# An eight-core attention and ternary-FFN layer on Trainium2: the loads of the down-projection weights are issued from GpSimd's queue instead of SyncE's and ScalarE's

## The reference, cut to what matters

```python
x = _layernorm(x + attn(x, Wq, bq, Wk, bk, Wv, bv, Wo, bo))     # 16 heads, 4 kv heads, RoPE, causal
# x: (2, 4096, 2048) float32; the FFN, on the normalised x:
def _quant_weight(w):                       # ternary weights
    scale = mean(|w|) + 1e-5
    return clip(round(w / scale), -1, 1) * scale
def _quant_act(x):                          # 8-bit activations, one scale a row
    scale = max(max|x|, 1e-5) / 127
    return clip(round(x / scale), -128, 127) * scale
gate = sigmoid(bitlinear(x, w_gate))        # w_gate, w_up: (8192, 2048)
up   = bitlinear(x, w_up)
h    = gate * up
y    = bitlinear(h, w_down)                 # w_down: (2048, 8192)
out  = _layernorm(x + y)
```

## Time and profile before

| | us |
|---|---|
| median of 3 runs | 6902.17 |
| the profiled execution, its own time | 6898.83 |
| its span on core 2, the slowest | 6897.1 |
| spans of the 8 cores | 6846.7 to 6897.1 |
| stage 5 on core 2, from the first weight DMA to the last `hscr` | 4077.4 to 5418.1 |
| PE busy in the whole span | 3070.9 (45%) |
| DVE busy | 2943.2 (43%) |
| ACT busy | 1663.0 (24%) |
| POOL busy | 386.1 (6%) |

### The profile page before, as it was taken

One profiled execution on the slowest core, in us unless ns is written; L12 is line 12 of the kernel. 1 busy time (PEld: TensorE's weight loads), 2 busy tenths in 40 slices (PEclk: granted clock), 3 DMA queues, 4 the chain that ended last, 5 costly groups with the idle time before them and its releaser, 6 DMA issues. The chain is left out here.

```text
span 6897.1 us, 49237 instructions; the slowest of 8 cores (6846.7 to 6897.1 us)
## 1 busy us (share of the span) xinstructions
PE 3070.9 (45%) x14187; PEld 1466.2 (21%) x14445; DVE 2943.2 (43%) x4502; ACT 1663.0 (24%) x2590; POOL 386.1 (6%) x747
## 2 busy tenths in 40 slices
PE   0014443133333445555546115777768344444442
PEld 0001111011112223333322002333323121222121
DVE  0015554365776555544431432434344433333333
ACT  0002222121223333333310211211112333333322
POOL 0001110121100000000000000000001000000000
PEclk9996776566555555555557557888889677777776
DMA  9977663677654333222224225665665502222202
GB/s 106 109 93 98 99 100 54 101 108 114 161 181 144 128 110 101 97 87 83 74 74 105 76 77 136 157 155 163 159 159 148 132 25 56 58 55 54 49 22 97
DMA packets 735830, 708.01 MB, mean 103 GB/s; under 512 B 607312, under 2 KB 607312, under 8 KB 705616
## 3 DMA queue, kind: packets, MB, share of 16 engines
q0 software_dynamic: 94768, 276.88, 21.0%
q1 hardware_dynamic: 580640, 268.57, 17.4%
q10 hardware_dynamic: 60160, 159.40, 7.3%
HBM read 545.28 MB, written 201.33 MB: 108 GB/s over the span
## 5 line engine op out<-in xcount | busy, mean ns | idle before, releaser
L1390 PE MATMUL gps<-wTg,xqTf 128*128 128x512 bf16 x1966 | 771.8, 393 | 340.3 <-DVE hb L1429 340.0
L1393 PE MATMUL ups<-wTu,xqTf 128*128 128x512 bf16 x2048 | 801.4, 391 | 52.5 <-DMA wTu<-wu_q 46.2
L950 PE MATMUL avp<-ptb,vsb 128*128 128x128 bf16 x2304 | 337.3, 301 | 705.4 <-DVE ptb L940 705.4
L398 DVE TENSOR_REDUCE asum<-mstage 128x1 f32<-128x1024 bf16 x384 | 451.0, 1214 | 269.4 <-DMA mstage<-wg 84.3
L1629 PE MATMUL dn<-wdT,hqT 128*128 128x512 bf16 x1998 | 537.2, 432 | 35.5 <-DVE acc L1648 21.1
L940 DVE COPY ptb<-ptp 128x512 bf16<-128x512 bf16 x576 | 243.8, 423 | 599.8 <-PE ptp L926 599.8
L999 ACT ACT_TABLE_LOAD x128 | 164.2, 1283 | 1182.7 <-remote 824.9
L465 PE MATMUL kps<-wkT,xtg 128*128 128x512 bf16 x491 | 227.0, 462 | 475.3 <-DMA xtg<-xkv_bf 475.1
L1415 ACT ACT_TABLE_LOAD x128 | 164.2, 1283 | 1101.1 <-DVE sgb L1404 1101.1
L926 PE MATMUL ptp<-ident,pnb 128*128 128x128 bf16 x2304 | 360.8, 311 | 136.0 <-DVE pnb L1028 134.3
L950 PEld LDWEIGHTS avp<-ptb,vsb 128*128 128x128 bf16 x2304 | 200.3, 127 | 842.4 <-issue 842.4
(11 more groups left out here) (228 smaller groups left out, 4097.5 us busy)
## 6 DMA issues: line engine op xcount, KB each, us to landing
mstage<-wg POOLq DMA_DIRECT2D x128, 256.0 KB, 6.6
mstage<-wu POOLq DMA_DIRECT2D x128, 256.0 KB, 5.9
mstage<-wd POOLq DMA_DIRECT2D x128, 256.0 KB, 5.4
wfsta<-wg SPq DMA_DIRECT2D x32, 1024.0 KB, 6.0
wfsta<-wg ACTq DMA_DIRECT2D x32, 1024.0 KB, 5.9
wg_q<-tbuf5a POOLq DMA_DIRECT2D x64, 512.0 KB, 5.7
wfsta<-wu SPq DMA_DIRECT2D x32, 1024.0 KB, 5.9
wfsta<-wu ACTq DMA_DIRECT2D x32, 1024.0 KB, 4.8
```

What stands on the lines that cost most here:

```text
L398: mt_red[t] = SM["vMi"].inc(v.reduce_sum(asum[:, t:t + 1], mstage(t)[:, 0:cw], AX.X, apply_absolute_value=True))
L950: last = te.matmul(avp[:, (u % 2) * 512:(u % 2) * 512 + 128], vsb[:, kb * KV + kvh * HD: kb * KV + kvh * HD + HD], ptb(gpar)[:, b * 128:(b ...
L1390: te.matmul(gps[:, qo:qo + 512], lhs, wTg(c)[:, j * 512:(j + 1) * 512], start=(j == 0), stop=(j == DC - 1))
L1393: last = te.matmul(ups[:, qo:qo + 512], lhs, wTu(c)[:, j * 512:(j + 1) * 512], start=(j == 0), stop=(j == DC - 1))
```

## The change

A set of four semaphores (`tfg`) is added. `fac_alloc` takes a flag; for stage 5 it is set, for stage 3 (which uses the same `emit_tern` for the gate and up weights) it isn't. With the flag, every load of a tile, even and odd, is issued by POOL and counted on `tfg` instead of `tf`. The number of buffers (four), the tiles, DVE's work and its place don't change.

```diff
-    def fac_alloc(stack, tag, nd=4):
+    def fac_alloc(stack, tag, nd=4, swdge=False):
         ...
+        FAC["swdge"] = swdge
@@ emit_tern
+        ld_sems = SP["tfg"] if FAC["swdge"] else SP["tf"]
         for t in range(lo, hi):
             wten, wscr, r0, c0, cw, ti = fac_tiles[t]
-            dec = B.sync if t % 2 == 0 else B.scalar
+            if FAC["swdge"]:
+                dec = B.gpsimd
+            else:
+                dec = B.sync if t % 2 == 0 else B.scalar
 
             @dec
             def _(eng, t=t, wten=wten, r0=r0, c0=c0, cw=cw, nd=nd):
                 if t >= nd:
                     eng.wait_ge(SM["vMi"].h, fac_mark[t - nd])
-                fac_ld[t] = SP["tf"][t % 4].inc(eng.dma_start(
+                fac_ld[t] = ld_sems[t % 4].inc(eng.dma_start(
                     wfst(t)[:, 0:cw], wten.ap()[r0:r0 + 128, c0:c0 + cw]), 16)
 
             @B.vector
-            def _(v, t=t, cw=cw, ti=ti):
-                v.wait_ge(SP["tf"][t % 4].h, fac_ld[t])
+            def _(v, t=t, cw=cw, ti=ti, ld_sems=ld_sems):
+                v.wait_ge(ld_sems[t % 4].h, fac_ld[t])
@@ stage 5
-        fac_alloc(p5, "b")
+        fac_alloc(p5, "b", swdge=True)
@@ end of stage 5
                 g.wait_ge(SP["tf"][3].h, SP["tf"][3].n)
+                g.wait_ge(SP["tfg"][0].h, SP["tfg"][0].n)
+                ...
```

More of the change, by code:

```diff
@@ L126, in build_nc @@
     SP["tf"] = [Sem(nc, st, "tf%d" % q) for q in range(4)]
+    SP["tfg"] = [Sem(nc, st, "tfg%d" % q) for q in range(4)]
     SP["tfw"] = [Sem(nc, st, "tfw%d" % q) for q in range(2)]
@@ L1473, in _ @@
                 g.wait_ge(SP["tf"][3].h, SP["tf"][3].n)
+                g.wait_ge(SP["tfg"][0].h, SP["tfg"][0].n)
+                g.wait_ge(SP["tfg"][1].h, SP["tfg"][1].n)
+                g.wait_ge(SP["tfg"][2].h, SP["tfg"][2].n)
+                g.wait_ge(SP["tfg"][3].h, SP["tfg"][3].n)
                 g.wait_ge(SP["tfw"][0].h, SP["tfw"][0].n)
```

## The result

The changed kernel takes 6743.07 us (median of 8 runs) beside 6902.58 for the kernel before: a ratio of 0.9775, 95% interval 0.9759 to 0.9791. The forecast was 6782. Run again beside other experiments it had 0.9761 (0.9749 to 0.9774). One execution each of e9 and e12, in which the cores of one die ran slower, is left out of their times and ratios.

What follows compares the result with a forecast made beforehand. DVE, held by the down-weight loads, was taken to bound stage 5. Tile 0's earlier start (64 us) and shorter intervals (53) save 117.0 from 6898.83, giving 6781.8, predicted as 6782; 8-in-10 range 6680 to 6885.

Steps and rivals of the forecast that it cites:

- The bound: Stage 5: PE is held by DVE (340.0 us) and DVE by the down-weight loads (584.0 us).
- The start of tile 0: Stage 5: DVE starts tile 0 at 4144.6 instead of 4208.7, saving 64 us.
- No load behind transposes, all prefetch lost: Stage 5: waits of 20.7 us a chunk and 70.33 at tile 0 end; every tile waits for its load.
- The wait of a load: Stage 5: DVE waits 7.40 us for each POOL load: 7.80 for ACT, less 0.90, plus 0.50.
- GpSimd's handicap: Stage 5 loads: a DMA by POOL may start slower, bounded at 0 and 1.0 us a load, taken as 0.5.
- The interval: DVE's time per tile in stage 5: 10.88 us own work plus 7.40 wait, 18.28 us; saves 53 us.
- Light collisions: Rival, chance 0.15: POOL's stage 5 loads meet transposes undisturbed; wait 5.11, interval 15.99, time 6638 us.
- heavy: Rival, chance 0.13: every stage 5 load costs as among transposes, full 1.0 us handicap; interval 19.78, time 6876 us.
- Slower: Rival, chance 0.07: POOL's stage 5 loads always jam among transposes; wait 9.86, interval 20.74, time 6937 us.
- PE's clock: Rival, chance 0.01: PE idles in stage 5 and its clock stays low; 27.5 us a tile, time beyond 7350.
- The weights of the chunks: Stage 5: SP's chunk weights keep up, 45 us of issue against a chunk of 73.

Runs made afterwards that it cites:

- e9: The changed kernel with each stage 5 load issued by GpSimd one tile ahead; 6512.44 us, 0.9445 of the kernel before.
- e12: Against the changed kernel, all tile loads issued by ScalarE, one iteration sooner, after hb of iteration 2t - 1; 6536.74 us, 0.9479 of the kernel before.
- e2: Against the changed kernel, all tile loads issued by ScalarE behind the sigmoid instead of by GpSimd; 6821.64 us, 0.9870 of the kernel before.
- e5: The changed kernel without the transposing loads of chunk weights from the fourth chunk on; 6684.47 us, 0.9670 of the kernel before.
- e6: As e2, all loads by ScalarE, but without transposing loads of chunk weights from the fourth chunk on; 6704.07 us, 0.9699 of the kernel before.
- e7: Against the changed kernel, all loads issued by ScalarE before the sigmoid, once hb of iteration 2t is done; 6678.57 us, 0.9668 of the kernel before.
- e3: The changed kernel with each load issued by GpSimd two tiles ahead; 6557.2 us, 0.9480 of the kernel before.

## Why the prediction was right, and what was mis-sized

- **The bound: right.** DVE, held by the loads, sets the stage, and PE follows. With the waits taken away (e9) PE is the bound, at 13.80 us a tile on its fastest core and 14.11 on its slowest; the forecast had 13.94.
- **The start of tile 0: right.** It begins 65.7 us after SP's first weight DMA (4135.90 less 4070.16), the forecast had 67.2 (4144.6 less 4077.43), before it was 131.3.
- **No load behind transposes, all prefetch lost: right.** 64 tiles wait where 46 did, none near 20 us. The sum on the slowest core is 435.1, the forecast "some 470".
- **The wait of a load: mis-sized, and the term is GpSimd's handicap.** The forecast was made for the slowest core and had 7.40; the slowest core of the changed kernel has 6.80 (435.1 / 64), the mean core 6.61. The 7.80 for ScalarE at that share of transposes was right: e2's slowest core measures 7.84, its mean core 7.51. GpSimd's issue was taken as 0.90 us sooner; it is 1.00. And GpSimd was taken as 0.5 us slower to deliver; among transposes, in its place behind `hscr`, it is not slower on the slowest cores (7.55 for 7.60) and 0.10 slower on the mean core. That term is some 0.5 of the 0.60 us by which the wait was over-priced. The forecast's lower bound for it (0) was the right value. What made 0.86 between e5 and e6, without transposes, is in part `hscr`.
- **The interval** on the slowest core is 17.81 us for 18.28, 29 us over 63 tiles, with single ones from 16.0 to 23.1 (forecast 16 to 21). The wait alone would have given 38 us; DVE's own part of an interval came out at 11.02 and not 10.88, which takes 9 back. The rest of the 39 us by which the time fell under the forecast is the place of tile 0, 9 us sooner than forecast, of which 7 lie ahead of stage 5: the slowest core is another one than before, and its stage began at 4070.16 and not 4077.43. Over all cores the start of the stage moved by 2 us only. So 7 of the 39 us are luck, a matter of which core is the slowest.
- **Light collisions** had an interval of 15.99, **heavy** 19.78: neither came. **Slower** needed a mean wait of 9.26; the longest single waits went down, not up.
- **PE's clock: the rival did not come, but "mostly 1.00" was wrong.** The forecast had PE waiting 4 us a tile at a clock near 1.00. On the slowest core it waits 2.7 (171.5 / 64) and its granted clock over the stage is 0.92. It is busy for 14.9 us a tile (951.55 / 64), where e9's slowest core at 0.98 to 1.00 needs 13.9 (859.75 us for 3968 matmuls, 64 a tile). That is hidden behind DVE.
- **The weights of the chunks: right.** 45 to 52 us of SP's issuing a chunk, which leaves 19 us or more in the 71 of a chunk, and PE waits for none of them after the first.

## What to carry to other kernels

A DMA in an in-order queue is as late as the last wait ahead of it: before moving it to another engine, write down the instant at which each queue would reach it and the instant at which it is needed. Here the change of queue took away a 20 us wait and left one of 6.6, since the new place is again just before the use; four buffers were paid for and one used. Moving the load one tile ahead on top of the change of engine gave 0.9445 where the engine alone gave 0.9775, and two tiles ahead in ScalarE's queue, with no load by GpSimd at all, 0.9509. Whether the old split between SyncE and ScalarE would have done as well with the loads moved ahead of the transposes was not run. And a load of GpSimd's that stood right behind writes in its queue landed later than one ahead of them (median 7.2 for 6.7 us behind 256 KB, 9.5 behind 768 KB).

## What the runs showed of the hardware that was not expected

- GpSimd started a DMA 0.54 us after the `hb` it waited for had ended, ScalarE 0.13 us after. With `hscr` ahead of it, that is a load 0.94 us later in e7's timeline, and the two kernels are 64 us apart.
- The granted clock was under full speed in long stretches in which PE hardly paused, on some cores (0.82 above). It happened in the changed kernel too, on cores 2 and 3. The windows are cores 2 and 3, then core 1 over the whole stage:

```profile
4140.00:4600.00 460.00, 442.76 (x1678) 183.76 (x1711) 213.12 (x259) 97.72 (x103) 56.03 (x104) 0.82 0.81 187
```
```profile
4140.00:4600.00 460.00, 435.30 (x1651) 178.24 (x1649) 204.83 (x250) 95.65 (x100) 53.92 (x100) 0.81 0.83 183
```
```profile
4078.00:5263.00 1185.00, 951.55 (x4096) 410.73 (x4096) 527.14 (x639) 244.80 (x256) 137.38 (x255) 0.92 0.71 169
```

- There it cost nothing that shows: core 2 has one of the shortest spans (6712.9 us), core 3 one of the longest (6739.4), and on both the interval is DVE's 11.0 to 11.1 us plus the wait for the load, as on the cores with a clock of 0.92 to 0.94. PE filled its pauses instead. A busy PE doesn't by itself bring the lower clock: e9's slowest core was busy for all of 410 us at 1.00. What does isn't known from these runs.

```profile
4600.00:5010.00 410.00, 410.00 (x1901) 185.85 (x1900) 240.31 (x298) 113.34 (x119) 64.22 (x119) 1.00 0.94 217
```

- Kernels bound by PE scatter more: e9's times go from 6490.93 to 6558.76 us and e3's from 6524.3 to 6589.94, the changed kernel's, run again in e9's company, from 6736.21 to 6758.86.
